# An axis-scan stage: GpSimd's order of work, its sent blocks and 35 of the 96 products

## The reference

```python
x1 = silu(causal_conv(x @ in_w)); delta = softplus(x1 @ dt_w + b)
dA   = einsum('bld,dn->bldn', delta, A)          # A in [-5, 0)
dB_u = einsum('bld,bld,bln->bldn', delta, x1, B)
c = exp(min(reversed_cumsum(dA[1:]), 15))        # over l
x = cumsum(dB_u * c, axis=1) / (c + 1e-6)
y = einsum('bldn,bln->bld', x, C) + x1 * D
out = (y * silu(res)) @ out_w
```

## Time and profile before

| | |
|---|---|
| median of 3 runs | 18923.57 us (18923.55 to 18954.09) |
| the profiled execution, own time | 18944.83 us |
| its span on the core | 18943.0 us |
| TensorE matmuls busy | 15897.0 us (84%) |
| VectorE busy | 16271.9 us (86%) |
| ScalarE busy | 15089.5 us (80%) |
| GpSimd busy | 14272.3 us (75%) |
| VectorE's scans | 1295.6 to 9116.6 us (first phase), 9348.7 to 17224.3 us (second), 64 each |

### The profile page before, as it was taken

One profiled execution on the slowest core, in us unless ns is written; L12 is line 12 of the kernel. 1 busy time (PEld: TensorE's weight loads), 2 busy tenths in 40 slices (PEclk: granted clock), 3 DMA queues, 4 the chain that ended last, 5 costly groups with the idle time before them and its releaser, 6 DMA issues. The chain is left out here.

```text
span 18943.0 us, 317228 instructions
## 1 busy us (share of the span) xinstructions
PE 15897.0 (84%) x72472; PEld 10167.4 (54%) x72568; DVE 16271.9 (86%) x43083; ACT 15089.5 (80%) x26177; POOL 14272.3 (75%) x11208
## 2 busy tenths in 40 slices
PE   8878888888888888888788888888888888887788
PEld 3335555555555555555455555555555555554233
DVE  7998888888888888888888888888888888887799
ACT  7768888888888888888688888888888888886488
POOL 4667777777777777777677777777777777776577
PEclk9999999999999999999899999999999999999899
DMA  1013333333333333333333333333333333333100
GB/s 40 16 22 64 61 61 63 58 64 62 61 63 59 63 63 60 65 60 60 53 65 60 63 61 60 63 60 65 58 63 62 62 61 60 64 61 59 23 15 14
DMA packets 1091289, 1050.17 MB, mean 55 GB/s; under 512 B 913376, under 2 KB 932476, under 8 KB 1089404
## 3 DMA queue, kind: packets, MB, share of 16 engines
q0 software_dynamic: 147456, 805.37, 22.2%
q1 hardware_dynamic: 938596, 221.43, 10.1%
q10 hardware_dynamic: 3352, 2.14, 0.1%
HBM read 152.05 MB, written 71.35 MB: 12 GB/s over the span
## 5 line engine op out<-in xcount | busy, mean ns | idle before, releaser
L1482 POOL TENSOR_TENSOR h_sm<-h_sm,h_wr 128x768 f32<-128x768 f32 x1664 | 3227.1, 1939 | 1574.1 <-DVE h_wr L1218 1302.5
L1482 POOL TENSOR_TENSOR w_sm<-w_sm,w_wr 128x768 f32<-128x768 f32 x1664 | 3212.3, 1930 | 1566.7 <-DVE w_wr L1218 1129.8
L1344 ACT ACTIVATE w_cbuf<-w_pe_e 128x1024 f32<-128x1024 f32 x2304 | 2358.5, 1024 | 1112.5 <-PE w_pe_e L1655 683.9
L1344 ACT ACTIVATE h_cbuf<-h_pe_e 128x1024 f32<-128x1024 f32 x2304 | 2358.8, 1024 | 1047.1 <-PE h_pe_e L1655 685.6
L1676 PE MATMUL h_pz<-h_xr,h_tri 128*128 128x384 f32 x6144 | 2769.9, 534 | 383.7 <-DVE h_sent L1218 238.7
L1676 PE MATMUL w_pz<-w_xr,w_tri 128*128 128x384 f32 x6144 | 2777.5, 535 | 364.8 <-DVE w_sent L1218 230.0
L1218 DVE SCALAR_TENSOR_TENSOR w_wr<-w_pz,w_bct,w_rbuf 128x192 f32<-128x192 f32 x6656 | 2415.8, 409 | 539.7 <-PE w_pz L1672 318.4
L1218 DVE SCALAR_TENSOR_TENSOR h_wr<-h_pz,h_bct,h_rbuf 128x192 f32<-128x192 f32 x6656 | 2414.1, 409 | 504.2 <-PE h_pz L1672 264.9
L1367 ACT ACTIVATE h_rbuf<-h_pe_e 128x1024 f32<-128x1024 f32 x2304 | 2365.0, 1027 | 33.8 <-DVE h_wr L1218 21.2
L1367 ACT ACTIVATE w_rbuf<-w_pe_e 128x1024 f32<-128x1024 f32 x2304 | 2364.6, 1026 | 34.1 <-DVE w_wr L1218 23.5
L1166 DVE SCALAR_TENSOR_TENSOR w_xr<-w_cbuf,w_bct,w_pdx 128x192 f32<-128x192 f32 x6144 | 2236.8, 405 | 40.8 <-PE w_pdx L1622 20.0
(11 more groups left out here) (381 smaller groups left out, 31803.0 us busy)
## 6 DMA issues: line engine op xcount, KB each, us to landing
h_held<-h_sent POOLq DMA_DIRECT2D x512, 768.0 KB, 6.0
w_held<-w_sent POOLq DMA_DIRECT2D x512, 768.0 KB, 5.8
h_lt<-pieces_s SPq DMA_DIRECT2D x512, 96.0 KB, 6.7
w_lt<-pieces_s SPq DMA_DIRECT2D x512, 96.0 KB, 7.5
pieces_s<-h_pieces SPq DMA_DIRECT2D x384, 48.0 KB, 2.1
pieces_s<-w_pieces SPq DMA_DIRECT2D x384, 48.0 KB, 2.1
h_xt<-first_s SPq DMA_DIRECT2D x34, 128.0 KB, 9.2
w_xt<-first_s SPq DMA_DIRECT2D x34, 128.0 KB, 7.4
```

What stands on the lines that cost most here:

```text
L1344: a.activation(cbuf[:, ch % 2, :, 64 * j:64 * j + 64].rearrange("p n (b d) -> p b n d", b=2), pe_e[:, G % 2 * 2:G % 2 * 2 + 2, :].rearrang ...
L1482: tt(sm[:, g], sm[:, g], wr[:, i % 3], ALU.add).then_inc(s_add, 1)
```

## The change

- `OTHER` has every P with P % 8 in (3, 5, 7): 35 pairs instead of 29. The six added (5, 21, 37, 53, 69, 85) leave `WIDE`.
- `SENT` becomes one tuple for each half: the first half has a sixth block (units 20 and 21), so it adds 11 units from the ring instead of 13 and has five sends instead of four.
- Held block and tree of the first half move from slots 22 and 23 to slot 34; those of the second half stand together in slot 47, behind all additions.
- Within a slot the order was addition, send, product, held block, tree, front step. It becomes front step, product, addition, send, held block, tree. The front steps keep their place against the additions but for `steps` and `make_dx`, which now go ahead of the product of slot 24.
- A send stands behind the first ring addition that comes after its two units (`CARRIER`). `wr` and `sent` go on from one half to the next instead of starting anew in each.
- VectorE's scan moves from behind pair 52 to behind pair 54, its gate from behind 57 to behind 58.

```diff
-        OTHER = [P for P in range(4, PAIRS) if P % 8 in (3, 7) or P % 16 == 13]
+        OTHER = [P for P in range(4, PAIRS) if P % 8 in (3, 5, 7)]
...
-        SENT = (0, 2, 4, 6, 8)
...
+        SENT = ((0, 2, 4, 6, 8, 10), (0, 2, 4, 6, 8))
+        KEPT = [[u for u in range(UN) if u // 2 not in SENT[g]] for g in range(2)]
+        TREE_AT = (34, 47)
+        RINGED = [(g, u) for g in range(2) for u in KEPT[g][1:]]
+        SENDS = [(g, b) for g in range(2) for b in SENT[g][1:]]
+        CARRIER = {}
+        for g, b in SENDS:
+            CARRIER[min((h, u) for h, u in RINGED if h * UN + u > g * UN + 2 * b + 1)] = (g, b)
+        SUMS = []
+        for U in range(2 * UN):
+            if (U // UN, U % UN) in RINGED:
+                SUMS.append(("add", U // UN, U % UN))
+            for g in range(2):
+                if TREE_AT[g] == U:
+                    SUMS += [("held", g, 0), ("held", g, 1), ("tree", g, 0)]
+        NA, ND = len(SUMS), len(SENDS)
+
+        def summed(what, g, n):
+            return SUMS.index((what, g, n)) + 1
...
-                            if P == 52:
+                            if P == 54:
                                 prefix(F)
-                            if P == 57:
+                            if P == 58:
                                 make_gate(F, q)
...
                 def add(T, g, u):
+                    if (g, u) in CARRIER:
+                        n = SENDS.index(CARRIER[g, u])
+                        if not (isinstance(T, int) and T == 0 and n == 0):
+                            pool.wait_ge(s_da, T * 16 * ND + n * 16)
                     pool.wait_ge(s_wd, T * PAIRS + g * 48 + 2 * u + 4)
+                    if ahead("add", g, u):
+                        pool.wait_ge(s_add, T * NA + NA + ahead("add", g, u))
+                    tt(sm[:, g], sm[:, g], wr[:, RINGED.index((g, u)) % 3], ALU.add).then_inc(s_add, 1)
...
-                        if u in KEPT[1:]:
-                            add(T, g, u)
-                        if u % 2 == 0 and u // 2 - 1 in SENT[1:]:
-                            send(T, g, SENT.index(u // 2 - 1))
-                        for P in OTHER:
-                            if (P - 7) // 2 == U:
-                                product(T, P)
-                        if u == LATE:
-                            add_held(T, g)
-                        if u == UN - 1:
-                            tree(T, g)
-                        if U == 10 and not first and not vertical:
-                            residual(T - 1, 1 - par, T * 6 + O_AT)
                         if not last:
                             if U == 24:
                                 steps(F)
                                 make_dx(F, q)
-                            if U == 26:
+                            if U == 27:
                                 suffix(F)
-                            if U == 29:
+                            if U == 30:
                                 remainder(F)
-                            if U == 31:
+                            if U == 32:
                                 piece3(F)
+                        for P in OTHER:
+                            if max((P - 7) // 2, 0) == U:
+                                product(T, P)
+                        if (g, u) in RINGED:
+                            add(T, g, u)
+                        if (g, u) in CARRIER:
+                            send(*CARRIER[g, u])
+                        for h in range(2):
+                            if TREE_AT[h] == U:
+                                add_held(T, h)
+                                tree(T, h)
+                        if U == 10 and not first and not vertical:
+                            residual(T - 1, 1 - par, T * 6 + O_AT)
```

More of the change, by code:

```diff
@@ L904, in phase_axis, with ahead @@
         OWN = PAIRS - len(OTHER)
-        SENT = (0, 2, 4, 6, 8)
[L907 to L912, removed]
-            if u == LATE:
[L914 to L917, removed]
+        SENT = ((0, 2, 4, 6, 8, 10), (0, 2, 4, 6, 8))
[16 more added lines that the diff above has]
+            return SUMS.index((what, g, n)) + 1
+        def ahead(what, g, n):
+            return max([i + 1 for i, x in enumerate(SUMS[:SUMS.index((what, g, n))]) if x[1] == g] + [0])
         def own(P):
@@ new lines, in place @@
+                    if u in KEPT[g]:
+                        return sm[:, g, at, :] if u == KEPT[g][0] else wr[:, RINGED.index((g, u)) % 3, at, :]
+                    k, at = SENT[g].index(u // 2), u % 2 * 4 + at
+                    return held[:, g, at, :] if k == 0 else sent[:, SENDS.index((g, u // 2)) % 2, at, :]
+                def room(T, g, u):
+                    first = isinstance(T, int) and T == 0
+                    if u in KEPT[g]:
+                        n = RINGED.index((g, u)) if u != KEPT[g][0] else None
+                        if n is not None and n >= 3:
+                            dve.wait_ge(s_add, T * NA + NA + summed("add", *RINGED[n - 3]))
+                        elif not first and n is not None:
+                            before = max(m for m in range(len(RINGED)) if m % 3 == n % 3)
+                            dve.wait_ge(s_add, T * NA + summed("add", *RINGED[before]))
+                        elif not first:
+                            dve.wait_ge(s_add, T * NA + summed("tree", g, 0))
+                    elif u % 2 == 0 and u // 2 == SENT[g][0]:
+                        if not first:
+                            dve.wait_ge(s_add, T * NA + summed("held", g, 1))
+                    elif u % 2 == 0:
+                        n = SENDS.index((g, u // 2))
+                        if n >= 2:
+                            dve.wait_ge(s_da, T * 16 * ND + (n - 1) * 16)
+                        elif not first:
+                            before = max(m for m in range(ND) if m % 2 == n % 2)
+                            dve.wait_ge(s_da, T * 16 * ND - ND * 16 + (before + 1) * 16)
@@ L1213, in weighted @@
                         dve.wait_ge(s_r, T * GRP + 3 * ch + 5)
-                    if P % 2 == 0 and not (isinstance(T, int) and T == 0 and g == 0 and u == KEPT[0]):
+                    if P % 2 == 0:
                         room(T, g, u)
@@ L1506, in tree @@
                 def tree(T, g):
-                    pool.wait_ge(s_add, T * 2 * NA + g * NA + 2 * NA - 1)
+                    pool.wait_ge(s_add, T * NA + NA + ahead("tree", g, 0))
                     tt(sm[:, g, 0:2], sm[:, g, 0:2], sm[:, g, 2:4], ALU.add).then_inc(s_tr, 1)
@@ L1629, in turn_y @@
                         pe.wait_ge(s_fe, f)
-                        pe.wait_ge(s_add, T * 2 * NA + 3 * NA)
+                        pe.wait_ge(s_add, T * NA + 2 * NA)
                     dst = pf[:, j * TB:(j + 1) * TB]
```

38 lines of the change are left out of this document (4 added, 34 removed).

## The result

The changed kernel takes 18636.8 us (median of 4 runs, 18624.37 to 18637.84), the kernel before, run beside it, 18927.62 us (4 runs): ratio 0.984, 95% interval 0.9825 to 0.9859. That is 291 us less, where 250 were forecast (18675). The profiled execution has a span of 18636.1 us.

What follows compares the result with a forecast made beforehand. Waits bound it, no engine full: VectorE for `steps`, then GpSimd's queue. Ordinary stage -4.7 - 0.5 + 1.6 + 1.8 + 0.3 = -1.5 us, every fourth -3.4; mean 2.0 over 126 stages gives 18675 us, range 18350 to 18940.

Steps and rivals of the forecast that it cites:

- `steps` without the work before it: First half, up to pair 61: `steps` starts earlier, VectorE no longer waits for it at the scan; -4.7 us a stage.
- the fast rival: Whole stage: ScalarE makes up time, landing 5.7 us, three products count; -4.8 us an ordinary stage, 18300 us; chance 0.15.
- ScalarE showing between 54 and 61: Sign against the forecast: VectorE waits for ScalarE, not GpSimd, between these pairs; no size given.
- Six products: Pairs 5, 21, 37, 53, 69, 85 go from VectorE to GpSimd; only 21 counts, -0.5 us a stage.
- from there to pair 7: GpSimd's queue from the addition of slot 42 to VectorE's pair 7: 24.2 us where it was 22.4, +1.8 us.
- Products ahead of additions: Second half, products of 91 and 93: VectorE's waits there go, but are worth nothing by themselves.
- Held block and tree in slot 34: Second half: pair 77 and the third send come later, so the addition of slot 42 starts 1.6 us later.
- the rival of a long landing: Addition of slot 42: third sent block needs 10.5 us to land, deciding from about 9.4; slower, 19025 us; chance 0.19.
- the clock term: TensorE's clock, a term of the ordinary stage's sum: +0.3 us.
- Every fourth stage: Stages with the decay-piece wait at pair 86, tied to pair 61: the later send costs nothing; -3.4 us.
- The sixth block: Slots 18 to 22: one more issue against two additions; at most 1 us at pair 94, covered by pair 5's wait.
- what the new profile should show: Signs: no `steps` wait; VectorE waits 2.3 us at 77, 4 to 6 at 5; third send some 23 after pair 61.

Runs made afterwards that it cites:

- 29 products: The changed kernel with the old list of GpSimd products, without the six added pairs: 18214.38 us, ratio 0.962.
- 5 and 7 first: The changed kernel with GpSimd's products of the next stage's pairs 5 and 7 ahead of held block and tree in slot 47: 17952.62 us, ratio 0.950.
- both moves: The changed kernel with products of 77 and 79 ahead of held block and tree in slot 34, those of 5 and 7 ahead in slot 47: 17921.25 us.
- order only: Against the changed kernel: five blocks, first tree in slot 23 behind `steps`, `make_dx`, product of 55; products of 5, 7 ahead of slot 47's tree: 18175.51 us.

## Why the prediction was right, and where its terms were off

The forecast of 250 us came out at 291, by the mechanism named: the wait for `steps` goes, and new waits at 77 and 5 give part of it back. That the two numbers are so near is luck in part. From 7 to 61 the stage is 6.1 us shorter where the terms say 5.2, and from 61 to 7 it is 3.7 longer where they say 3.2 in the mean of all stages; the two errors go opposite ways. Within 61 to 7 the price of the six products was put down to other terms.

- *`steps` without the work before it* (-4.7): right in kind, and a little small. 35 to 61 is 5.5 us shorter, of which 5.1 also come with the 29 products, between the 3.9 read from the rows and the 5.7 of the fast rival. The other 0.8 of the 4.7, also in the 5.7 (4.9 + 0.8), stood for the slow TensorE at the old wait (1.65 us for four matmuls in place of 0.82; granted clock 0.50 over these, 1.00 over the others); no run shows what it is worth by itself. What the traces show: in the kernel before, the four matmuls of pair 55 take 1.3 us in the mean of the 120 stages, after 3.9 us without work; in the changed kernel they follow other matmuls without a gap and take 0.82. Scan and ScalarE's copy stand as I placed them; a wait of 1.5 us for ScalarE's factors at the product of 54 is what is left. I said that ScalarE showing between 54 and 61 would make the forecast wrong. It does show there, by 1.5 us, and the forecast holds: the test was badly put, it needed a bound. What the step left out is that it depends on the tree's move: alone, the earlier `steps` is worth nothing (18938.55).
- *Six products* (-0.5): the term was right where I looked (7 to 35 is 0.5 shorter than with 29 products) and wrong as a price of the edit. It also took nothing for 37 and 53, and 35 to 61 is 0.4 shorter than with 29. Most of their 422 us lay in my term "from there to pair 7" (its 2.4 us from pair 5 to pair 7), which I booked under the queue: with pair 5 on the list the run ends at 5, and VectorE has two pairs still to do. The sum was right and the blame was not; a reader who wanted to improve the change by my list would have kept the six.
- *Products ahead of additions* ("worth nothing by themselves"): wrong in the changed kernel, 341 us. I judged the edit in the old order, where the products of 91 and 93 are the ones that it frees. In the new one it takes an addition away from before the product of 77 and a product from the run to 5.
- *Held block and tree in slot 34* (+1.6): pair 77 at 19.4 against 19.0 forecast, third send at 23.6 against 23.2. VectorE was there 0.5 us earlier than before (61 to 76 takes 15.9, not 16.4), so its wait is 3.4 us and not 2.4. The landing: I took 7.0 us, and over 60 stages its mean is 7.5 in the first phase and 6.9 in the second. It takes 8.8 us or more in 25 of these 120 stages but reaches the 9.4 at which the rival of a long landing decides in only two. The old landings took 8.5 and 10.1 us. So the addition of slot 42, counted from pair 61, starts 3.1 us later in the first phase and 0.8 in the second, against 1.6 forecast for both.
- *From there to pair 7* (+1.8, and +0.3 for TensorE's clock): the product of 5 starts at 48.9 after pair 61, I had 49.8 from an addition at 30.2 that in this stage started at 29.6. From it to the weighting of 5 takes 2.9 us, not 2.2, for the four matmuls take 1.64 us after 4.39 us without work where those of 77 take 0.91; so the clock term is 0.7 up to there, where the sum has 0.3 (my estimate; no run shows that value). It is the same slow TensorE as at the old wait, at the same granted clock of 0.50. 5 to 7 takes 3.0, not 2.4: the sum of pair 6 is still slow (1.49 us for its two matmuls, granted clock 0.50), and in the kernel with 5 and 7 first, where TensorE does not stand idle there and this sum takes 0.91 us at 1.00, it takes 2.4 (both as means too: 3.1 and 2.4). So I estimate the cost of the slow clock at this place at some 1.3 us (0.7, and 0.6 from pair 5 to pair 7). It shows at 77 as well, where I had no term for it: not in the worked stage (0.91 us), but in the mean of the 120 stages those four matmuls take 1.3 us after 3.2 us without work, and took 0.9 before. Pair 7 is weighted at 54.7 in this stage, as forecast (54.4 and 0.3), but its landing took 5.7 us and it is one of the shortest. In the first phase the ordinary stages of before take 4.9 us more from 61 to 7, where my terms add up to 3.7.
- *Every fourth stage*: "the wait for the decay pieces is tied to pair 61" was right in effect: this wait is nearly gone (300.2 us in both phases to 20.5), since pair 84 comes later. What it held is now held by the wait at 77. In the first phase these stages take 1.5 us more from 61 to 7, against 1.8 forecast. The sum leaves the clock's 0.3 out for them without a reason.
- *The sixth block* (at most 1 us at 94, covered): right, 18632.96 without it.
- *The second phase* gained 3.1 us a stage and the first 1.7. I used one value for both. GpSimd's waits for landings fell by 378 us in the second phase (407.9 to 29.7) and by 173 in the first (240.0 to 66.6). The third send's landing shows where it comes from: 3.1 us shorter than before in the second phase and 1.0 in the first. Of the 1.4 us between the phases 0.8 lie between 61 and 7, the rest between 7 and 35. That the image's transfers make the difference wasn't tested.

On what the new profile should show: wait for `steps` gone, right; 77 at 2.3, it is 3.8 in the mean; 5 at 4 to 6, it is 5.0 to 5.3; third send at 23, right; VectorE 2.8 less and GpSimd 2 to 3 more, right.

One such product takes 1.00 us on GpSimd (4131.61 above) and 0.54 on VectorE. With the changed kernel's order the six on GpSimd cost 422 us, but 3.1 of these 3.4 us a stage come from pair 5 being the one waited for and not from GpSimd's rate; with both moves the runs show no difference (5 us). Here the six products cost something only while the queue is waited for.

What remains open: what bounds the kernel with both moves. VectorE is busy 104 of 117 us, ScalarE 102, TensorE 102, and no pair has a mean wait of VectorE over 1.6 us. One thing points at the landing of the third send. The addition of slot 42 starts within 0.4 us of it in 110 of 120 stages; in the first phase the 30 stages whose landing takes 7.7 us or more last 118.8 us in the mean, the other 30 last 115.2. No run here makes that landing shorter, so it isn't shown.

## What to carry to other kernels

A long piece of work that nobody waits for soon (here 5.5 us of held block and tree) can set the length of the loop by what stands behind it in its engine's queue: list the next item behind it and who wants that, and put the item ahead. Moving the one that the profile names (`steps`, or the product of 77) only handed the wait to the next in line; the move that paid was the one at the end of a run of the queue without a gap. And price an edit with the others in place: the same six products cost 422 us or nothing, by where four other products stand.

## What the runs showed of the hardware

VectorE's scan and some of GpSimd's instructions took longer when they ran beside each other. In the kernel with order only, the scan starts 2.2 us into GpSimd's two additions of the held block and takes 2.31 us in place of 0.95, ending 0.8 us after they end; then the tree's first step takes 1.52 us in place of 0.99. It is so throughout: the median of the first phase's 64 scans is 2306 ns and that of the second's 2308, where it is 948 in both phases of the changed kernel. In the kernel before it was GpSimd's instruction that took longer: `make_dx`, started 0.05 us behind the scan (0.96 us), took 1.70 us (the median too) in place of 1.00. VectorE's weighting beside the same held block kept its 0.74 us, and the additions of the held block took 3.72 us, as in the kernel before (4134.98). What causes this isn't shown. The scan beside the held block is 1.4 us longer (2.31 less 0.95); how much of this is in the 1.8 us by which 35 to 61 is longer there wasn't tested. In the changed kernel GpSimd runs nothing beside the scan at 4106.13, and it takes 0.95 us; in this kernel I would place it so, and not beside the held block.
